# A vision tower with a routed feed-forward on one core: first loads in five pieces, later pieces held back, work of ScalarE regrouped

## Time and profile before

| what | us |
|---|---|
| median of 3 executions (lowest, highest) | 212.62 (211.5, 213.0) |
| profiled execution, its own time | 212.07 |
| its span, first to last instruction | 210.3 |
| PE busy, share of the span | 190.3, 91% |
| POOL busy | 138.1, 66% |
| DVE busy | 136.8, 65% |
| ACT busy | 127.1, 60% |
| mean granted clock of PE | 0.966 |

### The profile page before, as it was taken

How to read it: one execution, slowest core, us unless ns; L and a number is a source line. 1 busy time by engine, 2 the same in 40 slices (tenths; PEclk the granted TensorE clock), 3 DMA queues, 4 the chain that set the end, 5 groups by cost and what they waited for, 6 DMA issues and landing times.

```text
span 210.3 us, 4720 instructions
## 1 busy us (share of the span) xinstructions
PE 190.3 (91%) x1535; PEld 148.1 (70%) x1549; DVE 136.8 (65%) x422; ACT 127.1 (60%) x296; POOL 138.1 (66%) x186
## 2 busy tenths in 40 slices
PE   0599999999999789989999999999999999999940
PEld 0598999999999467647357676776776677766630
DVE  2889997649995882865677576878545554445420
ACT  0523567988279998989966656665443444444430
POOL 7699864499999951799989878788432322222222
PEclk9999999999999978997699999999999999999996
DMA  5999999859577772376767735744432122222111
GB/s 176 419 426 353 333 392 408 339 133 422 211 216 222 233 226 53 71 218 180 187 207 211 214 96 152 160 81 78 102 81 22 19 49 44 42 28 42 19 19 19
DMA packets 17152, 36.29 MB, mean 173 GB/s; under 512 B 2633, under 2 KB 7017, under 8 KB 16489
## 3 DMA queue, kind: packets, MB, share of 16 engines
q1 hardware_dynamic: 13753, 27.43, 41.6%
q0 software_dynamic: 2944, 2.76, 9.2%
q10 hardware_dynamic: 432, 5.80, 6.6%
HBM read 31.63 MB, written 4.36 MB: 171 GB/s over the span
## 4 chain that ended last, share of the span: by engine, by line
PE 75%; DMA 7%; ACT 7%; DVE 5%; issue 2%; POOL 1%; POOLq 1%; DVEq 0%; ACTq 0%
PE ps L1246 21%; PE ps L1467 6%; DMA experts<-x_t 5%; PE ps L1465 5%; PE ps L1477 5%; PE ps L1470 5%; PE ps L1469 5%; PE ps L1493 4%; PE ps L1495 4%; PE ps L1494 4%; PE ps L1466 3%; PE ps L1432 3%; ACT experts L701 2%; DMA out<-shared 2%; PE ps L1225 1%
## 5 line engine op out<-in xcount | busy, mean ns | idle before, releaser
L413 POOL TENSOR_TENSOR experts<-stage,experts 128x528 bf16<-128x528 f32 x48 | 56.7, 1212 | 16.4 <-ACT experts L666 16.2
L1246 PE MATMUL ps<-experts 128*117 128x193 f32 (+1 forms) x320 | 56.5, 336 | 8.1 <-DVE experts L932 7.7
L1246 PEld LDWEIGHTS ps<-experts 128*117 128x117 f32 (+1 forms) x320 | 54.1, 186 | 8.9 <-DMA experts<-x_t 8.7
L1178 DVE TENSOR_TENSOR shared<-shared,ps 128x256 f32<-128x256 f32 x48 | 20.2, 420 | 36.7 <-ACT shared L833 36.7
L666 ACT CAST experts<-stage 128x528 f16<-128x528 f32 x64 | 38.8, 632 | 1.7 <-DMA stage<-w_exp 1.7
L833 ACT ACTIVATE shared<-ps 128x256 f32<-128x256 f32 x48 | 18.4, 383 | 32.3 <-PE ps L1470 32.3
L648 ACT ACTIVATE experts<-experts 128x468 f32<-128x468 f32 x40 | 22.7, 590 | 17.8 <-POOL experts L506 6.5
L618 POOL DMA_INDIRECT out<-shared x8 | 12.4, 1545 | 29.8 <-ACT shared L858 27.1
L1493 PE MATMUL ps<-experts,shared 128*128 128x192 f16 (+1 forms) x96 | 23.6, 246 | 1.6 <-DVE shared L1183 1.6
L1494 PE MATMUL ps<-experts,shared 128*128 128x192 bf16 (+1 forms) x96 | 23.6, 246 | 0.0
L1495 PE MATMUL ps<-experts,shared 128*128 128x192 f16 (+1 forms) x96 | 23.6, 246 | 0.0
(11 more groups left out here) (230 smaller groups left out, 343.9 us busy)
## 6 DMA issues: line engine op xcount, KB each, us to landing
stage<-w_exp SPq DMA_DIRECT2D x64, 264.0 KB, 3.2
experts<-x_t ACTq DMA_DIRECT2D x3, 1888.0 KB, 9.8
experts<-w_proj SPq DMA_DIRECT2D x4, 768.0 KB, 7.6
experts<-x_t SPq DMA_DIRECT2D x4, 472.0 KB, 8.2
experts<-x_t SPq DMA_DIRECT2D x1, 1888.0 KB, 14.7
slot_x<-experts SPq DMA_DIRECT2D x1, 1032.0 KB, 6.0
shared<-slot_x SPq DMA_DIRECT2D x8, 129.0 KB, 2.3
out<-h SPq DMA_DIRECT2D x1, 351.0 KB
```

Source lines behind the costliest of these rows:

```text
L413: ops.tensor_tensor(lo_w[:, to + EW:to + EW + PW], stage[:, n % STAGES, :], hi_w[:, to:to + PW], ALU.subtract).then_inc(split_pool if on_p ...
L1246: last = mm(dst, xbuf[:, t % 2, k, 0:m], gw[:, k, :], start=k == 0, stop=k == KT - 1)
```

## The change

The four equal pieces of the weights and tile 0 become five (8, 8, 8, 4 and 4 slices), and tile 1 comes in two halves. SP loads three expert pieces, waits until tile 2 is in, and loads the others. On ACT the squares of tile 3 come ahead of `cosine(0)` and of three `high_parts`; from there to the routing ACT is one to three expert pieces behind its old list. The six choice copies move into steps 3 to 8, and `finish` of chunks 8 to 14 moves one step forward. POOL does two pieces fewer ahead of its marks (tile 3's squares, both `low_parts`) and one fewer ahead of the routing facts. DVE does `weighed(3)` and `weighed(4)` inside `normed(0)`. PE's unread products get new counts, `turn_back(2)` moves behind two `turn_queries`, and the products by fours go.

```diff
+        PARTS_K = [(0, 8), (8, 16), (16, 24), (24, 28), (28, KT)]
@@ SP
-            for j in range(4):
-                ks = slice(j * KC, (j + 1) * KC)
+            for j, (k0, k1) in enumerate(PARTS_K):
+                ks = slice(k0, k1)
                 sp.dma_start(wraw[:, ks, :], wsrc[:, ks, :]).then_inc(w_in[j], 16)
                 sp.dma_start(xbuf[:, 0, ks, :], x[0, :, ks, :]).then_inc(x0_in[j], 16)
-            sp.dma_start(xbuf[:, 1], x[1]).then_inc(x_in[1], 16)
+            for j in range(2):
+                ks = slice(j * KT // 2, (j + 1) * KT // 2)
+                sp.dma_start(xbuf[:, 1, ks, :], x[1, :, ks, :]).then_inc(x1_in[j], 16)
...
-            load_pieces(0, 2 * STAGES + 2)
+            load_pieces(0, 3)
+            sp.wait_ge(x_in[0], 16)
+            load_pieces(3, 2 * STAGES + 2)
@@ POOL
-            rests(0, 9)
+            rests(0, 7)
             square_adds(3)
...
-            rests(9, 36)
+            rests(7, 34)
             low_parts(0)
-            rests(36, 39)
+            rests(34, 37)
             low_parts(1)
-            rests(39, 43)
+            rests(37, 42)
...
-            rests(43, POOL_FIRST)
+            rests(42, POOL_FIRST)
@@ ACT
-            cosine(0, ctheta[0:TOK, :], theta_angle[1], theta_angle[0])
-            high_parts(7, 10)
             for j in range(NG):
                 squares(3, j, j + 1)
-                if j >= 2:
-                    high_parts(8 + j, 9 + j)
-                if j == 3:
+                if j >= 1:
+                    high_parts(6 + j, 7 + j)
+                if j == 4:
                     load_x(4)
+            cosine(0, ctheta[0:TOK, :], theta_angle[1], theta_angle[0])
             squares(4, 0, 3)
             cosine_of(0)
             for j in range(3, NG):
                 squares(4, j, j + 1)
-                high_parts(13 + j, 14 + j)
+                if j >= 4:
+                    high_parts(10 + j, 11 + j)
...
             load_table(ACT.Sin)
-            high_parts(27, 28)
+            high_parts(24, 26)
             cosine_of(1)
...
             attend(3)
-            high_parts(28, 30)
+            high_parts(26, 28)
             attend(4)
             weighed_out(3)
-            high_parts(30, 31)
+            high_parts(28, 29)
             weighed_out(4)
-            high_parts(31, 34)
+            high_parts(29, 32)
             outputs(3)
             outputs(4)
-            high_parts(34, 38)
+            high_parts(32, 36)
             rows(0)
             keep_h1(0)
-            high_parts(38, 40)
-            for i in range(3):
-                choice_copy(i)
+            high_parts(36, 39)
             rows(1)
             keep_h1(1)
-            for i in range(3, 6):
-                choice_copy(i)
-            high_parts(40, 44)
+            high_parts(39, 44)
...
-            high_parts(44, 47)
+            high_parts(44, 45)
...
-                if r == 2 and c:
+                if r == 2 and 1 <= c <= E:
                     finish(c - 1)
                 if high < NP * E:
-                    high_parts(high, high + 1)
-                    high += 1
+                    more = 2 if n in (0, 2) else 1
+                    high_parts(high, high + more)
+                    high += more
+                if 3 <= n < 3 + 3 * len(GROUPS):
+                    choice_copy(n - 3)
+                if r == 1 and c > E:
+                    finish(c - 1)
@@ DVE
-            normed(0)
-            weighed(3)
-            weighed(4)
+            normed(0, between=(3, 4))
@@ PE
-            embed(1, 0, KC)
+            embed(1, 0, KT // 2)
             square_sum(0)
-            embed(1, KC, KT)
+            embed(1, KT // 2, KT)
...
             scores(0)
-            keep_busy(7, 5)
+            keep_busy(7, 8)
             scores(1)
             weigh(0)
-            keep_busy(7, 2)
+            keep_busy(7, 3)
             scores(2)
             turn_back(0)
             weigh(1)
+            keep_busy(7, 2)
             turn_back(1)
             weigh(2)
-            keep_busy(5, 2)
-            turn_back(2)
-            keep_busy(5, 4)
+            keep_busy(5, 7)
             turn_queries(3)
             turn_queries(4)
+            turn_back(2)
...
             route(1)
             keep_busy(6, 4)
-            keep_busy_by_fours(6, 3)
...
-            keep_busy(4, 5)
+            keep_busy(4, 3)
             turn_rows(0)
             keep_busy(4, 2)
```

More of the change, by code:

```diff
@@ L293, in scratch @@
             return ps[0:TOK, SPARE_AT[g] + off:SPARE_AT[g] + off + n]
-        w_in = [sem(f"w_in{j}") for j in range(4)]
-        x0_in = [sem(f"x0_in{j}") for j in range(4)]
+        w_in = [sem(f"w_in{j}") for j in range(len(PARTS_K))]
+        x0_in = [sem(f"x0_in{j}") for j in range(len(PARTS_K))]
+        x1_in = [sem(f"x1_in{j}") for j in range(2)]
         x_in = [sem("x_in0"), sem("x_in1")]
@@ L388, in wait_added, with part_of @@
             eng.wait_ge(sq_used_vec if vec_ssq(t) else sq_used_pool, (NG - 1) * tiles_before(t) + j)
+        def part_of(k):
+            return next(j for j, (k0, k1) in enumerate(PARTS_K) if k0 <= k < k1)
         def wait_x(eng, t, j):
             if t == 0:
-                eng.wait_ge(x0_in[j], 16)
+                eng.wait_ge(x0_in[part_of(j)], 16)
+            elif t == 1:
+                eng.wait_ge(x1_in[2 * j // KT], 16)
             else:
-                eng.wait_ge(x_in[t % 2], 16 * ((t + 1) // 2))
+                eng.wait_ge(x_in[t % 2], 16 * (t // 2))
         def wait_split(eng, n):
@@ L638, in squares @@
                 for j in range(j0, j1):
-                    wait_x(sc, t, j * GS // KC)
+                    wait_x(sc, t, j * GS)
                     if j == 0 and t >= 2:
@@ L777, in _ @@
                 squares(4, j, j + 1)
-                high_parts(13 + j, 14 + j)
+                if j >= 4:
+                    high_parts(10 + j, 11 + j)
             load_table(ACT.Exp)
-            high_parts(21, 22)
+            high_parts(18, 19)
             turned(0)
@@ L783, in _ @@
             turned(2)
-            high_parts(22, 24)
+            high_parts(19, 21)
             attend(0)
-            high_parts(24, 26)
+            high_parts(21, 23)
             attend(1)
             weighed_out(0)
-            high_parts(26, 27)
+            high_parts(23, 24)
             attend(2)
@@ L860, in _ @@
             rows_high(0)
-            high = 47
+            high = 45
             for n in range(NSTEP):
@@ L930, in gains @@
                 dve.wait_ge(w_in[j], 16)
-                ks = slice(j * KC, (j + 1) * KC)
+                ks = slice(*PARTS_K[j])
                 v.tensor_tensor(gw[:, ks, 0:D], wraw[:, ks, :], spread(gcol[:, ks].rearrange("p (k o) -> p k o", o=1), 2, D),
@@ L959, in _ @@
             gains(3)
+            gains(4)
             v.tensor_tensor(e_valid[:, :, :], spread(e1[:, :].rearrange("p (o e) -> p o e", o=1), 1, TILES),
@@ L1088, in weighed, with normed @@
                 dve.wait_ge(o_ready, t + 1)
-            def normed(g):
+            def normed(g, between=()):
                 t0, t1 = GROUPS[g]
@@ L1099, in normed @@
                     root(g, step)
+                for t in between:
+                    weighed(t)
                 dve.wait_ge(vchain, steps[0])
@@ L1226, in keep_busy @@
                        start=True, stop=True)
-            def keep_busy_by_fours(bank, n):
-                for _ in range(n):
-                    for b in range(HB):
-                        r = slice(32 * b, 32 * b + 32)
-                        mm(ps[r, bank * BANK:(bank + 1) * BANK], before[:, r],
-                           spread(ones_b[:, :].rearrange("p (o c) -> p o c", o=1), 1, BANK // P), start=True, stop=True)
             def embed(t, k0, k1):
@@ L1241, in embed @@
                 for k in range(k0, k1):
-                    if k % KC == 0 and (t == 0 or k == 0):
-                        wait_x(pe, t, k // KC)
+                    if k == 0 or t == 0 and k in (k0 for k0, _ in PARTS_K) or t == 1 and k == KT // 2:
+                        wait_x(pe, t, k)
                         if t == 0:
-                            pe.wait_ge(gw_ready, k // KC + 1)
+                            pe.wait_ge(gw_ready, part_of(k) + 1)
                     last = mm(dst, xbuf[:, t % 2, k, 0:m], gw[:, k, :], start=k == 0, stop=k == KT - 1)
```

## The result

The changed kernel took 217.52, 219.84, 221.22 and 225.0 us (median 220.53), the kernel before 212.81 in four executions (211.5 to 213.59). The ratio is 1.028 (95% interval 1.021 to 1.035). The profiled execution is the one of 217.52, +5.45 on the 212.07 of before; the forecast for that comparison was 213.8, +1.7, and its range ended at 216.2.

What follows compares the result with a forecast made beforehand. The prediction took POOL's pieces and `gexp` to bound the experts' start and PE to set the pace from there; +2.5 at chunk 8's rows and -0.8 at the tail gave +1.7 on 212.07, so 213.8, range 209.9 to 216.2.

Steps and rivals of the forecast that it cites:

- The sign: Whole kernel: slower, some 214.3 us against the median, +0.8%; chances slower 0.3, faster 0.19, same 0.51.
- the first loads, -0.7: Embedding on PE: the waits of 0.27 us for tile 1 and 0.42 for tile 2 go, together -0.7.
- I price this at 0: SP's queue: pieces 3 on and tile 3's cast and load stand behind SP's new wait for tile 2; cost 0.
- POOL, piece 43, `gexp`: Expert pieces: POOL's run starts at 87.3 with 20 pieces left, piece 43 lands at 102.0, `gexp` at 102.6 against 101.54.
- the scatter: POOL before chunk 8: it waits for `choice_copy(5)`, ending at 128.7, and starts the scatter at 128.8, +2.8.
- The forecast's 2.0: PE at the experts' start: a gap of 2 to 3 us halves the clock, costing 2.0 us (bounds 0 and 3.4).
- let 0.3 come back: POOL between the scatter and the load of chunk 8's rows: shorter waits between the first outputs recover 0.3 us.
- The tail: Last outputs: `finish(14)` comes 1.9 us earlier, so the last output starts at 204.6 instead of 205.40, -0.8.
- copies taken away ahead of `gexp` bring nothing: ACT ahead of the experts: some 1.1 us of copies saved for the first group is hidden, since `gexp` waits for piece 43.
- Rival 3: Clock stays down at the experts: 3.4 us instead of 2.0, whole 215.2, or 216.1 with piece 43 landing long; chance 0.15.
- Rival 4: Embedding: SP's wait does nothing, tile 2 lands as before, -0.3 instead of -0.7, whole 214.2; chance 0.05.
- and if tile 3 came late: Embedding: should tile 3 land late, PE would wait by that much; priced at 0.

Runs made afterwards that it cites:

- a_blanks: The changed kernel with SP's two blank writes issued two pieces earlier, after piece 13 instead of 15: 218.05 us, ratio 1.025 to the kernel before.
- a_nohold: The changed kernel without SP's wait for tile 2, so pieces 3 and on are issued at once: 216.86 us, ratio 1.020 to the kernel before.
- b_copies: The kernel before with only the six choice copies moved into steps 3 to 8 of the experts: 215.83 us, ratio 1.017.
- a_warm: The changed kernel with 18 instead of 2 unread products after `turn_rows(0)`: 215.18 us, ratio 1.013 to the kernel before.
- b_tail: The kernel before with only `finish` of chunks 8 to 14 one step earlier: 211.04 us, ratio 0.994.
- b_copwarm: The kernel before with the six choice copies in steps 3 to 8 and 8 instead of 2 unread products after `turn_rows(0)`: 214.98 us, ratio 1.010.
- b_ordwarm: The kernel before with the new lists of expert pieces on ACT and POOL and 14 instead of 2 unread products after `turn_rows(0)`: 215.78 us, ratio 1.015.

## Why the prediction was wrong

The sign was right, and so was the shape: no gain at the experts' start, a long gap, a cold clock, a scatter behind the last copy, an earlier tail. Step by step, the profiled execution beside the forecast:

| step | forecast | measured |
|---|---|---|
| attention starts, against before | -0.7 | +0.7 |
| POOL's unbroken run | 87.3 | 88.88 |
| `gexp` | 102.6 | 104.11 |
| first expert product | 106.4 | 107.75 |
| PE idle before it | 2 to 3 | 4.0 |
| cost of the slow clock | 2.0 | 1.9 to 2.4 |
| `choice_copy(5)` ends | 128.7 | 130.63 |
| scatter starts | 128.8 | 131.69 |
| chunk 8's rows turned | +2.5 | +6.2 |
| tail | -0.8 | -0.8 |

- **The step that failed first is "the first loads, -0.7", with the hold at "I price this at 0".** PE's waits for tiles 1, 2 and 3 went as forecast, but the 0 was said of pieces 3 on, and for these I asked only whether tile 3 comes in time. I did not ask what else stands in SP's queue behind the hold and behind GpSimd's splits: the blanks and piece 16. The 1.36 us wait goes when the blanks go early (a_blanks) and also when the hold goes (a_nohold). The swing of 1.4 went nearly unchanged to POOL's run (+1.6), piece 43, `gexp` (+1.5) and the first product (+1.35), as a ring of stages passes on what it gets. That much of the chain "POOL, piece 43, `gexp`" stood, only later. But this step isn't the whole: with 0.94 of it mended, a_blanks still turns chunk 8's rows 5.6 us late. The larger part failed in the step "the scatter" and behind it.
- **The scatter.** The forecast had it start 0.1 us after the copy. It starts 1.06 to 1.07 after, in the change and in every run with late copies; the earlier trace rows have 0.70 behind POOL's own operation, and I should have put that after the copy too. This is 1.0 of the error. The copies also push each other's steps: `silu(8)` is 17.70 us behind the first product in b_copies (124.19 - 106.49), 17.44 in before (123.83 - 106.39). In the change it is 20.08 (127.83 - 107.75), so the clock costs 20.08 - 17.70 = 2.4, or 20.08 - 18.22 = 1.9 by a_warm, which has the changed kernel's own steps. The forecast's 2.0 is met, but by luck: it was the price of tile 0's slow start, and there the granted clock is 1.00 in all of 7.7 to 20 us, so those rows don't show a fallen clock.
- **What reached chunk 8.** The forecast let 0.3 come back between the scatter and the load. POOL's ten scatters and first outputs gave nothing back but lost 0.8: from the scatter's +5.7 the load was +6.5. Up to the tenth scatter POOL's waits did shrink, by 0.2, but its thirteen instructions for indirect transfers ahead of it took 17.6 us where they had taken 16.6; why is open. PE's spare time took a little of that, +6.2.
- **The sum of errors at chunk 8's rows**, 3.7: 1.35 from the first loads, 1.0 from the scatter's start, 0.6 from the steps up to the last copy (the clock and the copies in them; the shares aren't settled), and 0.8 from what came back or didn't.
- **The tail** was right to a tenth; b_tail has it at 0.6% in all.
- **That copies taken away ahead of `gexp` bring nothing** held: without them there `gexp` is at 101.77 in b_copies, where it waits 1.06 us for DVE's ranks behind a slow routing, and at 102.01 in b_copwarm, where ACT waits 2.07 us for the stage instead; it was 101.54.
- **Rivals.** Rival 3 put the decision in the right place, the gap before `gate_up(0)`, with a price of +1.4 for it; what made the change slower than the range is in no rival. Rival 4 fell: tile 2 does come without a wait. That the hold would cost was in the forecast as a place ("and if tile 3 came late") and not as a case.

The 5.45 us are the profiled execution, the change's fastest. The medians are further apart, and of those others there is no profile. b_copies and b_copwarm show one source of such a spread, a clock that falls in the routing in one execution and at the experts in another. The second fall, behind the wait for chunk 8's rows, is another: the change's fastest execution escaped it, a_blanks and a_nohold did not. That the slower executions of the change have it isn't shown.

Alone, hold, copies and order cost 1.1, 1.7 and 1.5%, and the tail gives 0.6; that would be 3.7, and 2.8 was measured. With intervals of 0.4 to 0.6 on each side for the parts and 0.7 for the whole, these numbers don't show that the costs overlap. The traces make it likely: the copies and the order both hold the scatter, and the later of the two counts.

## What to carry to other kernels

When a wait is put into a queue, or a step is moved ahead of the one that frees its buffers, list everything issued behind it on that queue up to the next place with slack, whatever it is for; the blank writes here had nothing to do with pieces or tiles. Keep work that one late, expensive step needs off the lists of a pipeline whose pace can vary: copies that were free ahead of the experts came to carry the clock's moods to the scatter. A gap in TensorE's work that opens ahead of dense products can have a second price behind the gap (1.9 to 2.4 us at the experts, 1.7 at chunk 8's rows), so count products nobody reads anew whenever the work before them gets faster. And when a repair brings less than its wait was long, read the trace behind the repaired place before the reading is dropped: the rest may be lost again further on, as in a_blanks.

## What the runs showed of the hardware

**GpSimd's small operations end late where VectorE's lie over them.** POOL's operation of L583 takes 0.57 us in the kernel before and 0.20 in b_copies. The kernel before, first DVE, then POOL:

```profile
121.01 0.70 DVE L413 TENSOR_TENSOR experts<-stage,experts 128x528 bf16<-128x528 f32 x1
...
122.29 0.89 DVE L1150 TENSOR_TENSOR yy<-slot,slot_val 117x640 f16<-117x640 f32 x1
```
```profile
121.20 0.57 POOL L583 TENSOR_TENSOR cexp<-cexp,pow 128x8 f32<-128x8 f32 x1
...
122.23 1.08 POOL L587 TENSOR_TENSOR posm<-hot,val 117x40 f32<-117x40 f32 x2
```

POOL's operation at 121.20 ends at 121.77, just behind DVE's at 121.71, and the pair from 122.23 ends at 123.31, behind DVE's end at 123.18. In b_ordwarm DVE's split of 120.27 to 121.10 stands over a POOL operation of 120.49 to 121.16 (0.67 instead of 0.21), and six of POOL's pieces took 7.85 us there where 6 x 1.16 are 7.0. So the time between the facts and the scatter would depend on how many of DVE's operations of this kind fall on POOL's. The Trainium skill (SBUF — State Buffer, section "SBUF: two separate sides") states that VectorE and GpSimd share a pair of ports, and that a VectorE operation with two SBUF inputs and a GpSimd operation that reads SBUF lock each other out of it, the one that starts first for its whole instruction; the ends of these rows agree. No experiment took DVE's work away from there, so that it is the whole of the missing 1.2 us in b_ordwarm is argued, not shown.

**The clock falls in different places in executions of the same kind of work.** The routing, 96 to 102 us, ran at 0.50 in b_copies and at 1.00 in b_copwarm, with nothing changed ahead of it. The kernel before is exposed to the same and hides it: it fell at 97 in its profiled execution, in b_tail at 106 to 108, and all executions of both lie within 2 us of their medians. At chunk 8's rows it fell behind PE's waits of 2.08 us (a_blanks) and 2.32 us (a_nohold), and stayed at 1.00 behind the one of 1.87 us in the change.
